# A graph network on one core: comparisons against numbers in PSUM, turned attributes through the second sum bank, norms per five tiles

## The reference, cut to what matters

```python
x = x + gnn(layernorm(x))         # attention: softmax over each node's edges, weighted sum of h[col]
x = x + ffn(layernorm(x))         # top-k tokens by a router, 256 -> 1024 -> 256, gelu
x = x + gcn(layernorm(x))         # three layers, below
x = x + moe(layernorm(x))         # gate from the mean over all rows, 2 of 8 experts, 256 -> 512 -> 256
...
ew = edge_attr @ edge_w + edge_b                   # 32 attributes per edge -> 256
for l in range(3):
    msg = relu(x[src] * ew)
    out = x @ roots[l] + biases[l]
    for i in range(3):                             # edge types
        h = segment_sum(msg * mask[i], dst) * inv_cnt[i]
        out = out + h @ weights[l, i]
    x = x + relu(out)
```

## Time and profile before

| | us |
|---|---|
| median of 3 runs | 5876.84 (5876.79 to 5910.19) |
| the profiled execution | 5877.75 |
| its span, first to last instruction | 5875.9 |
| PE busy | 4422.1 (75%) |
| DVE busy | 4128.0 (70%) |
| POOL busy | 4095.9 (70%) |
| ACT busy | 2287.6 (39%) |
| mean granted TensorE clock | 0.901 of full speed |

### The profile page before, as it was taken

The page is one execution under the profiler, slowest core; times in us unless marked ns, Lnnn a source line. Parts: engine busy times, 40 slices in busy tenths (PEclk is TensorE's granted clock), DMA queues, the critical chain, the costliest instruction groups (busy, mean ns, idle before and its releaser), DMA issues.

```text
span 5875.9 us, 87690 instructions
## 1 busy us (share of the span) xinstructions
PE 4422.1 (75%) x24964; PEld 2778.1 (47%) x24964; DVE 4128.0 (70%) x9409; ACT 2287.6 (39%) x5880; POOL 4095.9 (70%) x4202
## 2 busy tenths in 40 slices
PE   4399987888888695767777767777776777777787
PEld 2255544666666463444444434444444444444455
DVE  7899886777777735676676657776775777777734
ACT  0088775555555423333333323333332233232321
POOL 4567777777777777777777757777776777777700
PEclk6599997889888798998999989999998899999978
DMA  5011102333333215444444434544444444444400
GB/s 162 15 51 28 27 25 78 105 105 107 102 105 103 76 28 149 134 136 129 134 132 127 130 108 138 139 139 139 138 139 116 139 138 140 137 139 139 136 21 22
DMA packets 442666, 624.95 MB, mean 106 GB/s; under 512 B 94683, under 2 KB 327920, under 8 KB 442223
## 3 DMA queue, kind: packets, MB, share of 16 engines
q0 software_dynamic: 187648, 457.52, 28.0%
q1 hardware_dynamic: 250164, 159.14, 9.6%
q10 hardware_dynamic: 4414, 2.96, 0.2%
HBM read 556.32 MB, written 62.94 MB: 105 GB/s over the span
## 4 chain that ended last, share of the span: by engine, by line
PE 24%; DVE 13%; issue 12%; POOL 11%; ACT 2%; DVEq 2%; DMA 2%; POOLq 0%; ACTq 0%; SPq 0%
PE banks L1160 13%; POOL sort_mem L625 8%; DVE acc_mem L1679 6%; DVE z_mem L1822 5%; PE banks L1190 4%; POOL recB_d L583 3%; PE banks L1148 2%; PE banks L1093 1%; PE banks L1103 1%; DMA sort_mem<-x_d,x_mem 1%; DVEq L1668 1%; ACT z_mem L815 1%; DVEq L1679 1%; PE banks L1145 1%; PE banks L1180 1%
## 5 line engine op out<-in xcount | busy, mean ns | idle before, releaser
L625 POOL DMA_INDIRECT sort_mem<-x_d,x_mem x2568 | 2455.3, 956 | 885.5 <-issue 759.9
L1160 PE MATMUL banks<-z_mem 128*128 128x257 f32 x5136 | 1578.5, 432 | 902.8 <-DVE acc_mem L1679 767.2
L1160 PEld LDWEIGHTS banks<-z_mem 128*128 128x128 f32 x5136 | 858.5, 200 | 1601.8 <-ACT z_mem L815 719.0
L1679 DVE TENSOR_TENSOR acc_mem<-acc_mem,banks 128x257 f32 x2568 | 1079.7, 420 | 564.0 <-PE banks L1160 390.0
L815 ACT ACTIVATE z_mem<-z_mem 128x512 f32<-128x512 f32 x1284 | 768.6, 628 | 1388.0 <-DVE z_mem L1822 1388.0
L1822 DVE TENSOR_TENSOR z_mem<-banks,sort_mem 128x512 f32<-128x512 f32 x1284 | 825.0, 685 | 412.9 <-PE banks L1148 295.0
L592 POOL DMA_INDIRECT acc_mem<-h_d,xnt_mem x808 | 801.3, 992 | 246.1 <-issue 231.8
L583 POOL DMA_INDIRECT recB_d<-acc_mem,sort_mem x680 | 712.7, 1048 | 320.0 <-issue 205.5
L1036 PE MATMUL banks<-acc_mem,xnt_mem 128*128 128x257 f32 x1616 | 569.8, 476 | 46.6 <-DVE acc_mem L1622 44.8
L1622 DVE SCALAR_TENSOR_TENSOR acc_mem<-acc_mem,z_mem,banks 128x257 f32 x808 | 386.2, 478 | 112.8 <-PE banks L1036 98.3
L1148 PE MATMUL banks<-z_mem,x_mem 32*128 32x256 f32 x5136 | 427.3, 409 | 0.0
(11 more groups left out here) (348 smaller groups left out, 5549.6 us busy)
## 6 DMA issues: line engine op xcount, KB each, us to landing
x_mem<-recB_d SPq DMA_DIRECT2D x642, 68.0 KB
sort_mem<-x_d,x_mem POOLq DMA_INDIRECT x2568
x_mem<-at_d SPq DMA_DIRECT2D x428, 64.0 KB
at_d<-x_mem SPq DMA_DIRECT2D x214, 64.0 KB
acc_mem<-h_d,xnt_mem POOLq DMA_INDIRECT x808, 2.8
x_mem<-x_d SPq DMA_DIRECT2D x100, 128.0 KB, 2.9
acc_mem<-in_edge_attr SPq DMA_DIRECT2D x40, 312.5 KB
recB_d<-acc_mem SPq DMA_DIRECT2D x3, 3672.0 KB, 28.6
```

What stands on the lines that cost most here:

```text
L625: pool.indirect_dma_start(out=xg[h % XG][:, k, :], out_offset=None, in_=x_ds[l % 2], in_offset=bass.IndirectOffsetOnAxis(ap=reci[h][:, k, ...
L1160: m.matmul(bank[5 + tile % 2][:, :AC], oneh[:, Q % 2, k, :], msg[:, Q % 2, k, :], start=True, stop=True)\
L1679: v.tensor_tensor(a_, a_, bank_[:, :AC], ALU.add).then_inc(flushed, 1)
```

## The change

1. **Numbers in PSUM.** `numbers`, a float32 copy of `iota` in the last quarter of bank 7, takes the place of `iota_b` in `late_onehot`, `hot_columns` and `one_hots`; one copy at the start, and a wait for the late ranks (which use the rest of bank 7) ahead of `one_hots`. `column_numbers` in bank 4 serves all three layers.
2. **Layer one's turned attributes.** PE's `turn` of quad Q + 4 moves from behind the sums of Q to between the third and the fourth of them, into the last quarter of bank 6 (the second sum bank). The copy to SBUF moves from ACT to DVE, between flushes 2 and 3. The first four go through bank 5 ahead of the loop.
3. **Norms per five tiles.** At both products a new `normalize` runs whenever five token tiles are done, with an inverse square root by four Newton steps on DVE (`inverse_std`, 15 operations of 128 x 5) in place of ACT's square root and a reciprocal; at the end tiles 20 to 23 and tile 24 apart. The norm after the layers stays as it was. SP's stores of the state go between those of x2, the fifth at feed 4.
4. **Clears in two parts.** ACT clears the windows that don't overlap the edge records' room (20 of 25) as soon as x2 is done, and waits for the scatters only ahead of the rest. DVE's wait for the clears moves behind quad 1's multiplications.
5. **Mean over the rows.** 25 products of a column of ones with a tile's 256 columns, a scale on DVE, two turns on PE and a copy, in place of 50 products with one column each.
6. PE's wait for the scaled experts' weights moves behind the first two `up`.

```diff
+        column_numbers = bank[4][:, 0:P]
+        turned_attr = bank[6][:, 3 * P:4 * P]
+        numbers = bank[7][:, 3 * P:4 * P]
...
             for t0 in range(0, NT, 5):
                 sp.wait_ge(S("x2_group"), t0 // 5 + 1)
...
+                if t0 + 5 < NT:
+                    store_state(t0 // 5)
...
             for Q in range(TURN):
                 feed(0, Q)
-                if Q < 3:
-                    store_state(Q + 2)
+                if Q == LAG - 1:
+                    store_state(4)
...
             act.wait_ge(S("x2_ready"), 1)
-            for u in range(4):
-                act.wait_ge(S(f"edges_put{u}"), BODIES // 4 * 320)
             for i in range(NT):
+                if R * i * AC <= EREC < R * (i + 1) * AC:
+                    for u in range(4):
+                        act.wait_ge(S(f"edges_put{u}"), BODIES // 4 * 320)
                 clear_windows(R * i, R)
...
-                def copy_attr(Q, h, n):
-
-                    act.wait_ge(S("rec_turned"), Q + 1)
...
-                    a.activation(at[:, h, :], bank[4][:, h % 4 * P:(h % 4 + 1) * P], ACT.Copy).then_inc(S("attr_ready"), 1)
...
                 up(0, 512)
                 up(1, 512)
+                if n:
+                    pe.wait_ge(S("moe_w_scaled"), 1)
                 down(0, 0, 512)
...
+                        if l == 0 and k == 3 and Q + 4 < QB:
+                            turn(Q + 4, turned_attr)
                         m.matmul(bank[5 + tile % 2][:, :AC], oneh[:, Q % 2, k, :], msg[:, Q % 2, k, :], start=True, stop=True)\
...
-                    if l == 0 and Q + 4 < QB:
-                        turn(Q + 4)
...
-                for k in range(2):
-                    last = m.matmul(bank[4 + k][:, 0:1], x_sb[:, tt, k * P:(k + 1) * P], ones[:, 0:1],
-                                    start=(tt == 0), stop=(tt == NT - 1))
+                last = m.matmul(bank[4][0:1, :D], ones[:, 0:1], x_sb[:, tt, :], start=(tt == 0), stop=(tt == NT - 1))
+            last.then_inc(S("rows_summed"), 1)
+            pe.wait_ge(S("mean_ready"), 1)
+            for k in range(2):
+                last = m.matmul(bank[5][:, k:k + 1], ycol[0:1, 0, k * P:(k + 1) * P], ones[0:1, 0:1], start=True, stop=True)
...
+            st.did(v.tensor_copy(numbers, iota))
...
-                v.tensor_tensor(seg1[:, o % 3, :, :], iota_b.rearrange("p (a s) -> p a s", a=1).broadcast_to([P, 8, P]),
+                v.tensor_tensor(seg1[:, o % 3, :, :], numbers.rearrange("p (a s) -> p a s", a=1).broadcast_to([P, 8, P]),
...
+            def inverse_std(lo, hi):
+
+                var, inverse = sd[:, lo:hi], rs[:, lo:hi]
+                half = root[:, :hi - lo]
+                st.settle()
+                st.run(v.tensor_scalar(var, mv[:, lo:hi, 1], EPS, None, ALU.add))
+                st.run(v.tensor_single_scalar(half.bitcast(INT32), var.bitcast(INT32), 1, ALU.logical_shift_right))
+                st.run(v.tensor_scalar(inverse.bitcast(INT32), half.bitcast(INT32), -1.0, float(0x5f3759df), ALU.mult, ALU.add))
+                for _ in range(4):
+                    st.run(v.scalar_tensor_tensor(half, inverse, -0.5, inverse, ALU.mult, ALU.mult))
+                    st.run(v.tensor_tensor(half, half, var, ALU.mult))
+                    st.run(v.scalar_tensor_tensor(inverse, half, 1.5, inverse, ALU.add, ALU.mult))
+
+            def normalize(dst, src, lo, hi):
+
+                inverse_std(lo, hi)
+                for tt in range(lo, hi):
+                    st.did(v.tensor_scalar(dst[:, tt, :], src[:, tt, :], mv[:, tt, 0:1], rs[:, tt:tt + 1],
+                                           ALU.subtract, ALU.mult))
+                st.settle()
...
                 norm_stats(x_sb, tt)
-            st.settle()
+                if tt % 5 == 4:
+                    normalize(xn, x_sb, tt - 4, tt + 1)
+                    dve.sem_inc(S("state_ready"), 1)
             dve.sem_inc(S("x2_ready"), 1)
 
-            layer_norm(3, xn, "state_ready", stats_made=True, group=5, order=NORM_ORDER)
...
-                column_numbers = bank[4][:, :P] if l else iota
+                def copy_attr(Q):
+
+                    h = Q % TURN
+                    dve.wait_ge(S("rec_turned"), Q + 1)
+                    if Q >= TURN:
+                        dve.wait_ge(S("projected"), Q - TURN + 1)
+                        dve.wait_ge(S(f"at_moved{h}"), Q // TURN * 16)
+                    v.tensor_copy(at[:, h, :], turned_attr).then_inc(S("attr_ready"), 1)
...
                         flush_B(Q - 1, 2, wins)
+                        if l == 0 and Q + 3 < QB:
+                            copy_attr(Q + 3)
                         flush_B(Q - 1, 3, wins)
...
+                if tt % 5 == 4 and tt < NT - 1 or tt >= NT - 2:
+                    lo = tt // 5 * 5 if tt < NT - 1 else tt
+                    normalize(x_sb, x_sb, lo, tt + 1)
+                    xx, oo = x_sb[:, lo:tt + 1, :], xn[:, lo:tt + 1, :]
+                    st.run(v.tensor_tensor(xx, xx, vecs[:, 2:3, :].broadcast_to([P, tt + 1 - lo, D]), ALU.mult))
+                    st.run(v.tensor_tensor(oo, oo, xx, ALU.add))
+                    dve.sem_inc(S("out_ready"), 1)
```

82 lines of the change are left out of this document (34 added, 48 removed).

## The result

| | before | after |
|---|---|---|
| median of 4 runs each | 5889.56 (5876.79 to 5910.19) | 5741.47 (5738.37 to 5744.57) |
| the profiled execution | 5877.75 | 5738.37 |
| its span | 5875.9 | 5736.6 |

A forecast was written before the change was run, and what follows sets the result against it. In most of the successive stages POOL's indirect DMAs were taken to set the pace, with DVE, PE and ACT as slow in layer one. The terms summed to -115.5 us from 5877.75, giving 5762 us, range 5720 to 5828.

The forecast's parts named there:

- Numbers in PSUM, gather: Gather stage: with the comparison's numbers in PSUM, POOL's DMAs fall to layer two's mean; -29 us (-10 to -37).
- inference from two places of the trace: Gather stage: two DMAs ended 0.82 and 0.84 us after DVE operations with two SBUF inputs, so these seem to hold POOL.
- 5.63 us row: A DMA started at 2005.30 in a run of L1686 and ended 0.84 us after it, after 5.63 us.
- rival of another cause: Pair, gather, layer one: stretched DMAs don't come from two SBUF inputs, so the stretching stays; 5812 us, chance 0.06.
- Pair stage: -8 forecast: Pair stage: comparisons with numbers in PSUM delay POOL's 440 DMAs less; -8 us (+5 to -25).
- POOL is waited for in the second half alone: Pair stage: only there does ACT's make_records wait, 76.1 us, for POOL's DMAs; POOL's whole loss was put at 21 us.
- Layer one: -45 forecast: Layer one: lower POOL floor and earlier ACT relu cut a quad from 5.30 to 5.09 us; -45 us (0 to -71).
- 60% of ACT's 75 us: Layer one: share taken of the gain from quads with a wait on ACT, as plain quads gain nothing; -45 us.
- A gain in layer one near 67: Layer one: sign that the turn costs nothing and POOL alone sets the layer's pace.
- rival that the other engines take over: Gather and layer one: ACT, PE and DVE set the pace, gains only -10 and 0; 5826 us, chance 0.17.
- The start of layer one: -9 forecast: Ahead of layer one: norms per five tiles and earlier ACT clears bring the first multiplication forward; -9 us (0 to -11).
- The end: -24.5 forecast: Kernel's end: final norms beside the product -14.5, mean over the rows -7.5, later wait for scaled weights -2.5 us.

The follow-up runs named there:

- run with plain rows in the old order: Kernel before, with three of each quad's four indirect gathers in layer one made plain DMAs of other rows; 5871.8 us.

## Why the prediction was right, and where its sizes were off

*Numbers in PSUM, gather: -29 forecast.* Right in mechanism and size. POOL's work shrank by 37.5 us, 8.4 of them came back as idle time, and POOL's stage is 29.1 us shorter (1047.1 to 1018.0). What was an inference from two places of the trace is shown by the runs in layers two and three: either operand in PSUM gives 946 to 948 ns, both in SBUF 983 to 991. The Trainium skill (SBUF — State Buffer, "Who interferes with whom") says that a VectorE instruction with two SBUF inputs contends with a GpSimd instruction that reads SBUF. That agrees with these runs, if an indirect DMA, which takes its rows by a list in SBUF, counts as one. The forecast also took its 5.63 us row as evidence against an inference of the Trainium skill in the same section, that tensor_tensor leaves the generation of descriptors alone. There the forecast read too much into the row: L1686 is a scalar_tensor_tensor, and what it held is an indirect DMA. In the run with plain rows in the old order, plain DMAs that POOL issued inside a tensor_tensor with two SBUF inputs weren't held:

```profile
2822.67 0.68 DVE L1813 TENSOR_TENSOR z_mem<-iota,x_mem 128x512 f32<-128x512 f32 x1
2822.99 1.63 POOL L626 DMA_DIRECT2D sort_mem<-x_d  x3
```

Over that layer 81 of them started 0.05 to 0.45 us into a comparison and took 0.54 to 0.59 us, as all others did, while an indirect DMA that started in a tensor_tensor with two SBUF inputs took up to 1.94 us in the gather stage of the kernel before. Which part of an indirect DMA waits wasn't tested. The rival of another cause is out.

*Pair stage: -8 forecast, -19.1 in the profile.* POOL's loss was sized rightly: 21 us by the estimate, 440 x (1054 - 1008) ns = 20 in the traces. The step that failed is "POOL is waited for in the second half alone", from which only a part of the 21 was counted. POOL works through a queue of scatters without a pause in both halves: its work and its own issue time, 463.8 and 133.5 us, fill the stage's 597. What it loses in the first half makes the queue longer, and that is waited for in the second. Four profiles shown above give it almost us for us: with 455.7, 477.1, 484.2 and 498.4 us of scatters the gather starts at 916.9, 937.3, 944.2 and 958.3. If an engine has a backlog, all of its loss reaches the end, also from the time in which nobody yet waited.

*Layer one: -45 forecast, with -9 for its start; -65.3 measured.* The parts were named rightly: a floor that POOL's shorter DMAs lower, and a chain that is shortened. The step that failed is "60% of ACT's 75 us", from 5.30 to 5.09 us a quad: the chain falls to 4.76, so that POOL's floor decides alone. The prediction had named that sign itself ("A gain in layer one near 67"). With POOL out of the way the chain lost 107 us, more than all of ACT's 75. Putting ACT's wait back cost 47 of them, close to the 45 taken, but that closeness is luck: the 47 are measured with the turn at its new place, which had already cut PE's wait for ACT from 83.9 to 28.2 us. The forecast charged the turn 0.3 us at its new place and credited it nothing for leaving its old one, where it kept both ACT and the projection waiting. The copy was free, as taken: 283 ns on DVE, in a layer that DVE doesn't bound.

Both halves of the change are needed: with the comparison alone in SBUF again layer one takes 1141.4 us, with the chain as before some 1160 (an estimate: the old order took 1161.1 without POOL's pace), with both in place 1097.7. The rival that the other engines take over is out: they have a small part in the gather, and none of the weight in layer one that it gave them.

*The start of layer one: -9 forecast, -2.1 measured.* The first multiplication comes 12.8 us after POOL's first gather, instead of 14.9. The timeline after (DVE's last norm group, ACT's clears, POOL's first gather, DVE's first multiplication), as the earlier trace rows:

```profile
2193.33 1.72 DVE L1459 TENSOR_SCALAR xnt_mem<-x_mem,small 128x256 f32<-128x256 f32 x5
2195.24 18.77 ACT L784 ACTIVATE acc_mem<-small 128x771 f32<-128x771 f32 x26 [24.12 <-DVEq L1801]
2205.00 0.97 POOL L628 DMA_INDIRECT sort_mem<-x_d,x_mem  x1 [8.15 <-issue]
2217.81 1.29 DVE L1840 TENSOR_TENSOR z_mem<-banks,sort_mem 128x512 f32<-128x512 f32 x2 [0.87 <-PE banks L1137]
```

ACT's clears start when the norm is done (2195.05), 3 us before the last scatter has landed (DVE goes on at 2198.19) and not 9 us before it, as forecast. In the kernel before the last token tile had been done 14 us before the last landing (2231.23 to 2245.24), now it is 8 us (2190.16 to 2198.19). The compute up to that tile gained 41 us, while POOL's scatters gained 47. The step that failed is that the forecast took the old distance of 14 us between the two. It cost nothing, as POOL sets layer one's pace from its first gather on. In the two profiles with the numbers in SBUF the first multiplication came 7 us after the first gather, instead of 12.8, and layer one still took 1100.6 and 1099.1 us. So the item had no value of its own.

*The end: -24.5 forecast, -24.8 measured.* PE's products of the mean, PE's first up, tile 23's last statistics, and the last addition on DVE after the change, as the earlier trace rows:

```profile
L1199 PE MATMUL banks<-x_mem,ones 128*1 128x256 f32 x50 | 13.5, 438 | 7.2 <-DVEq L1440 7.2
5545.87 14.38 PE L1082 MATMUL banks<-xnt_mem,acc_mem 128*128 128x512 f32 x28 [1.48 <-DMA vecs<-in_L_ffn_b]
5718.58 0.18 DVE L1420 BATCH_NORM_AGGREGATE small<-small 128x2 f32<-128x6 f32 x1
5731.69 0.42 DVE L1981 TENSOR_TENSOR xnt_mem<-xnt_mem,x_mem 128x256 f32<-128x256 f32 x1
```

From the first product of the mean to the first up of the experts' product it is 8.0 us less (43.0 to 35.0), where 10 were forecast for the mean and the scaled weights: the wait for the scaled weights is gone, but behind it the load of the experts' biases is late (1.48 us before the first up). The final norm ends 186.2 us after the first up instead of 201.1, -14.9 against -14.5, and the smaller last store gave 1.9 more.

## What to carry to other kernels

Where GpSimd's indirect DMAs set the pace, look for VectorE operations with two tensors from SBUF beside them, and bring one of the two (a constant, or a few columns) through PSUM: here it cost VectorE nothing and gave 20 to 44 us a stage. When two engines are equally late, take each out of the way once: in layer one POOL out of the way alone gave 1.9 us (1163.0 to 1161.1), the new order alone 21.6 (to 1141.4), and both parts of the change together 65.3. An engine that works off a backlog passes on every loss, so size it over the whole time that the backlog exists.
